# Scores of the large cross-attention stages from rounded keys and queries and their rests, in three passes

## The reference, cut to what matters

```python
q = (h @ Wq).reshape(B, N, 16, 64)        # h: layer norm of x, 112 tokens
k = (context @ Wk).reshape(B, S, 16, 64)  # 375 positions
v = (context @ Wv).reshape(B, S, 16, 64)
scores = einsum('bnhd,bshd->bhns', q, k) * scale
attn = softmax(scores)                    # over the 375 keys
x = x + einsum('bhns,bshd->bnhd', attn, v).reshape(B, N, 1024) @ Wo + bo
```

## Time and profile before

| | us |
|---|---|
| median of 3 runs | 1735.83 (1734.51 to 1738.16) |
| the profiled execution, its own time | 1738.72 |
| its span, first to last instruction | 1736.9 |
| mean granted clock of TensorE | 0.979 |

### The profile page before, as it was taken

One profiled execution on the slowest core, in us unless ns is written; L12 is line 12 of the kernel. 1 busy time (PEld: TensorE's weight loads), 2 busy tenths in 40 slices (PEclk: granted clock), 3 DMA queues, 4 the chain that ended last, 5 costly groups with the idle time before them and its releaser, 6 DMA issues.

```text
span 1736.9 us, 37112 instructions
## 1 busy us (share of the span) xinstructions
PE 1625.8 (94%) x13752; PEld 1378.1 (79%) x13752; DVE 978.4 (56%) x2648; ACT 1027.5 (59%) x2824; POOL 556.1 (32%) x1016
## 2 busy tenths in 40 slices
PE   5799999999989999999999979999999988999977
PEld 5788888888778888887888779888887777777757
DVE  6656644444656656644445555644455577767644
ACT  4456665566743556665556643555556676677771
POOL 3754333232221534333223220433223213443300
PEclk9899999999999999999999999999999999999989
DMA  4430210001110100210001110200101100111000
GB/s 131 148 113 31 66 33 14 14 15 52 42 36 29 62 1 26 72 33 15 15 14 41 42 43 30 67 17 15 28 15 48 52 17 4 32 30 31 2 4 19
DMA packets 37873, 65.07 MB, mean 37 GB/s; under 512 B 6784, under 2 KB 12384, under 8 KB 37696
## 3 DMA queue, kind: packets, MB, share of 16 engines
q1 hardware_dynamic: 37696, 62.70, 11.4%
HBM read 57.15 MB, written 5.54 MB: 36 GB/s over the span
## 4 chain that ended last, share of the span: by engine, by line
PE 81%; DVE 6%; ACT 6%; issue 3%; POOL 2%; DMA 1%; SPq 0%; DVEq 0%; POOLq 0%; ACTq 0%
PE pG L989 49%; PE pG L1119 12%; PE pS L989 10%; PE pO L989 10%; ACT L1309 1%; ACT P L1261 1%; DVE KF L1398 1%; ACT PT L1274 1%; ACT hid_lo_f L1309 1%; PE pG L1172 1%; DVE x L1441 1%; DMA V<-ctxT 1%; DVE bn L1324 1%; POOL P L1510 0%; DVE tmp L1439 0%
## 5 line engine op out<-in xcount | busy, mean ns | idle before, releaser
L1510 POOL TENSOR_SCALAR P<-P,rinv 112x375 f32<-112x375 f32 (+1 forms) x640 | 325.6, 520 | 565.6 <-DVE rinv L1404 565.3
L1261 ACT ACTIVATE P<-pS,nmax 112x375 f32<-112x375 f32 (+1 forms) x640 | 306.4, 492 | 212.4 <-DVE nmax L1380 212.2
L989 PE MATMUL pG<-hT_hi,W 128*128 128x224 f32 (+1 forms) x1408 | 336.5, 317 | 27.4 <-POOL hT_lo L1544 15.6
L989 PEld LDWEIGHTS pG<-hT_hi,W 128*128 128x128 f32 x1408 | 251.6, 201 | 38.4 <-issue 16.5
L1380 DVE TENSOR_REDUCE nmax<-pS 112x1 f32<-112x375 f32 (+1 forms) x448 | 229.3, 548 | 92.1 <-PE pS L989 91.7
L1274 ACT ACTIVATE PT<-pG 125x336 f32<-125x336 f32 (+1 forms) x448 | 208.0, 467 | 110.6 <-PE pG L1119 108.5
L1119 PE MATMUL pG<-ident,P 112*125 112x112 f32 (+1 forms) x1472 | 240.8, 277 | 18.0 <-POOL P L1510 8.4
L989 PE MATMUL pG<-src,W 128*128 128x376 f32 x1120 | 244.8, 349 | 0.3 <-DVE hid_hi_f L1357 0.3
L1119 PEld LDWEIGHTS pG<-ident,P 112*125 112x125 f32 (+1 forms) x1472 | 200.6, 176 | 53.7 <-issue 11.1
L989 PE MATMUL pG<-W,src 128*125 128x512 f32 x840 | 232.7, 410 | 1.0 <-DVE hid_lo_t L1365 0.7
L989 PE MATMUL pG<-hT_lo,W 128*128 128x224 f32 (+1 forms) x704 | 215.6, 306 | 0.0
(11 more groups left out here) (97 smaller groups left out, 2409.6 us busy)
## 6 DMA issues: line engine op xcount, KB each, us to landing
wraw<-wts SPq DMA_DIRECT2D x116, 256.0 KB, 2.5
src<-ctx_split SPq DMA_DIRECT2D x64, 282.0 KB, 3.0
ctx_split<-hid_lo_t SPq DMA_DIRECT2D x8, 564.0 KB, 4.0
V<-ctxT SPq DMA_DIRECT2D x8, 376.0 KB, 4.1
V<-wts SPq DMA_DIRECT2D x8, 256.0 KB, 3.4
bo_b<-bo SPq DMA_DIRECT2D x10, 112.0 KB, 2.7
out<-x SPq DMA_DIRECT2D x8, 112.0 KB, 1.8
x<-x_in SPq DMA_DIRECT2D x1, 672.0 KB, 5.5
```

The lines of the kernel that those rows point to most:

```text
L989: return nc.tensor.matmul(o, l, r, start=first, stop=last)
L1261: ins = act.activation(o, pS[U % 4][0:T, i * n:(i + 1) * n], ACT.Exp, bias=nmax[:, r, i:i + 1], accum_out=rsum[:, r, i:i + 1])
L1510: ins = pool.tensor_scalar(o, o, rinv[:, r, i:i + 1], st.nscale, ALU.mult, ALU.mult)
```

## The change

In stages 1 and 3, and in stage 4 from batch 2 on (`split`), the float32 score matmul of each head becomes three float32r matmuls: rounded queries with rounded keys, rounded queries with the keys' rest, the queries' rest with rounded keys. Only the product of the two rests is left out. For this

- VectorE copies a key tile from PSUM into a place for rests (`keys_rest`) instead of into `KF`; GpSimd rounds it into `KF_hi` (same memory as `KF`) and subtracts that in place;
- ScalarE scales a query tile into `queries_rest` instead of `QF`; VectorE rounds it into `QF_hi` (same memory as `QF`) and subtracts that in place (`ql`, two operations with a wait between);
- the rests lie in the feed-forward tiles, behind their tiles 0 and 1, so the first writes wait until these are free (`rest_free`), and hidden tiles 2 to 7 of the last batch wait until the sets that read the rests there are scored (`HID_FREE`);
- the pairs of hidden tiles in the last batch's four fills become 3, 1, 2 and 2;
- the planner's costs follow.

```diff
+def split(s, b):
+    return s in (1, 3) or s == 4 and b > 1
+HID_FREE = {0: 0, 1: 0, 2: 1, 3: 2, 4: 3, 5: 3, 6: 4, 7: 4}
...
-            for t in ((0, 1, 2), (3, 4), (5, 6), (7,))[i]:
+            for t in ((0, 1, 2), (3,), (4, 5), (6, 7))[i]:
...
-            return 1.25 if st.self_ else .7 if st.small else 1.75
+            return 1.25 if st.self_ else .7 if st.small else 1.2 if split(e.s, e.b) else 1.75
...
+        rest = nc.alloc_sbuf_tensor_at("rest", [128, 16 * CHUNK], F32R, offset=place)
+        whole_f = nc.alloc_sbuf_tensor_at("whole_f", [128, 16 * CHUNK], F32, offset=place)
...
+        def keys_rest(t, of=rest):
+            a = 2 * CHUNK + t // 2 * (SP + PAIR) + t % 2 * 8 * CHUNK
+            return of[:, a:a + SP]
+        def queries_rest(t, of=rest):
+            a = 2 * CHUNK + t // 2 * (SP + PAIR) + t % 2 * 8 * CHUNK + SP
+            return of[:, a:a + PAIR]
+        def rest_free(eng, s):
+            if s == 1:
+                wait(eng, ctx_out, 16 * B)
+            else:
+                wait(eng, pieces, piece_no[Ev("ff2", 1 if s == 3 else 3, B - 1)])
...
@@ tensor, set @@
-                                if st.small:
+                                if st.small or split(s, b):
                                     wait(pe, k_split, split_no[Ev("k", s, b, t)])
...
+                        if split(s, b):
+                            for p in range(3):
+                                for u in us:
+                                    t, r = sh.heads(u)[0]
+                                    rg = slice(rows * r, rows * (r + 1))
+                                    q = queries_rest(t)[rg, qc] if p == 2 else QF_hi[rg, t, qc]
+                                    k = keys_rest(t)[rg, :] if p == 1 else KF_hi[rg, t, :]
+                                    ins = mm(pS[u % 4][0:T, 0:SP], q, k, p == 0, p == 2)
...
@@ scalar, q @@
+                        if split(s, 2 * b):
+                            rest_free(act, s)
+                            o = queries_rest(e.i, whole_f)
+                        else:
+                            o = QF[:, e.i, :]
...
@@ scalar and vector, hidden tiles @@
+                    elif s < 6:
+                        rest_free(act, s)
+                        if HID_FREE[e.i]:
+                            wait(act, scored, scored_after(s, B - 1, 2 * HID_FREE[e.i] - 1))
...
@@ vector, k and ql @@
+                    elif split(s, b):
+                        wait(dve, scored, keys_free(s, b, e.i))
+                        rest_free(dve, s)
+                        dve.tensor_copy(keys_rest(e.i, whole_f), g[:, 0:SP]).then_inc(k_ready, 1)
...
+                    if not st.small:
+                        dve.tensor_copy(QF_hi[:, e.i, :], queries_rest(e.i, whole_f)).then_inc(q_hi, 1)
+                        dve.wait_ge(q_hi, q_hi_no[e])
+                        dve.tensor_tensor(queries_rest(e.i), queries_rest(e.i, whole_f), QF_hi[:, e.i, :].bitcast(F32),
+                                          ALU.subtract).then_inc(ql_ready, 1)
...
@@ gpsimd, k @@
+                    if s < 6:
+                        t = e.i
+                        pool.tensor_scalar(KF_hi[:, t, :], keys_rest(t, whole_f), 1.0, 1.0, ALU.mult, ALU.mult).then_inc(k_part, 1)
+                        pool.wait_ge(k_part, n)
+                        pool.tensor_tensor(keys_rest(t), keys_rest(t, whole_f), KF_hi[:, t, :].bitcast(F32), ALU.subtract).then_inc(k_split, 1)
```

More of the change, by code:

```diff
@@ L389, in duration @@
             return .62 if st.small else .6
-        return dict(ta=.75, tb=.68, hn=.42, ql=.36, w=.58, stat=.75, k=.55, qk=.72, norm=.15, wo=1.6, ff2=1.6, lnt=.78, ctx=.5, ffa=1.65, ffg=1.1)[k]
+        return dict(ta=.75, tb=.68, hn=.42, ql=.5, w=.58, stat=.75, k=.55, qk=.72, norm=.15, wo=1.6, ff2=1.6, lnt=.78, ctx=.5, ffa=1.65, ffg=1.1)[k]
     if k == "norm":
@@ L480, in plan @@
                 else:
-                    needs += [evicted(Ev("q", s, b // 2, t)), ("pool" if s == 6 else "dve", Ev("k", s, b, t))]
+                    needs += [("dve", Ev("ql", s, b // 2, t)) if s == 6 or split(s, b) else ("act", Ev("q", s, b // 2, t)), ("pool" if s == 6 or split(s, b) else "dve", Ev("k", s, b, t))]
             needs += [read(unit_no(s, b, u) - 4) for u in us if unit_no(s, b, u) > 3]
@@ L495, in plan @@
             task("act", e, ("pe", e))
-            if e.kind == "q" and s == 6:
+            if e.kind == "q" and (s == 6 or split(s, 2 * b)):
                 task("dve", e._replace(kind="ql"), ("act", e))
-        elif e.kind == "k" and s == 6:
+        elif e.kind == "k" and (s == 6 or split(s, b)):
             task("dve", e, ("pe", e))
@@ L651, in program @@
     ql_no = number(order["dve"], "ql")
+    q_hi_no = number([e for e in order["dve"] if e.s < 6], "ql")
     split_no = number(order["pool"], "k")
@@ L1097, in _ @@
                         bank_read(pe, unit(e, us[-1]) - 4)
-                        for i in range(sh.G if s < 6 else 0):
+                        if split(s, b):
[6 more added lines that the diff above has]
+                                    ins = mm(pS[u % 4][0:T, 0:SP], q, k, p == 0, p == 2)
+                        for i in range(sh.G if s < 6 and not split(s, b) else 0):
                             for u in us:
@@ L1475, in _ @@
                         wait(dve, pieces, piece_no[Ev("ff2", s, 3)])
-                    elif s == 3:
-                        wait(dve, pieces, piece_no[Ev("ff2", 1, B - 1)])
-                    elif s == 6:
+                    elif s < 6:
+                        rest_free(dve, s)
+                        if HID_FREE[e.i]:
+                            wait(dve, scored, scored_after(s, B - 1, 2 * HID_FREE[e.i] - 1))
+                    else:
                         dve.wait_ge(scored, scored_after(6, B - 1, 2 * (e.i - 4) + 1) if e.i > 3 else scored_after(6, B - 2, 7))
```

19 lines of the change are left out of this document (10 added, 9 removed).

## The result

The changed kernel takes 1756.5 us (median of four runs, 1755.6 to 1762.3) where the kernel before takes 1736.6 beside it: a ratio of 1.0122, 95% interval 1.0098 to 1.0147. It is slower by 20 us by the medians, 21 by the ratio; the forecast was faster by 20. The profiled execution is the one of 1762.3 us, 6 above the other three, so terms read from its trace come out somewhat large against the medians.

What follows compares the result with a forecast made beforehand. TensorE's own work was taken to bound the steady batches. Score sets -22.9, openings +2.8 and feed-forward pairs 0 sum to -20.1 us, from 1735.8 to 1715.7 us, range 1708 to 1728.

Steps and rivals of the forecast that it cites:

- The set: Score sets of stages 1, 3 and 4: 1.19 us each instead of 1.45, 22.9 us gained over 88 sets.
- The rival of the weight loads: Score sets: two weight loads per step go one after the other, step 187 ns, 1727.3 us; chance 0.08.
- The heads do run side by side: Score sets: the rival had heads not side by side in float32r, 2.26 us per set, 1810 us; chance 0.03.
- the third term: Last batch's feed-forward pairs, 3, 1, 2, 2: 0 us, between a gain of 2.5 and a loss of 3.2 per stage.
- the waits for hidden tiles: Last batch's feed-forward: hidden tiles wait for sets that TensorE has already gone through; cost nothing.
- The key copy keeps its form, only its target moves, and ScalarE's query eviction too: nothing.: Evictions from PSUM on VectorE and ScalarE in the converted stages: no added cost.
- Two covers: Converted stages: 7.3 us from norm to transpose and about 9 us from tile to set hide the splits.
- The sign of being right: Steady windows: TensorE stays over 99% busy and they get shorter by some 0.26 us per set.
- The query's split on VectorE: 88 query tiles, copy and subtraction within SBUF: 0.7 us each (0.4 to 0.85), 62 us in all, VectorE half idle.
- its GpSimd rival: Odd batches: key splits ahead of norms make GpSimd late, VectorE possibly held up to 1.0 us; 1773 us, chance 0.05.
- The openings: Last batches of stages 0 and 2: next stage's key splits delay norms, 2.8 us lost in all (0 to 6).
- the chance of 0.08 for slower: Whole kernel: chance of being slower by over 0.2%, about what a measurement can tell.

Runs made afterwards that it cites:

- the passes at the old costs: Kernel before with only the score sets as three float32r passes, rests left out, planner's old costs: 1715.2 us with old pairs, 1714.8 with new.
- old costs: Changed kernel with the planner's old cost of a set (1.75) and of the small stage's query rest (0.36): 1743.9 us, 1.0044.
- the deferrals: Changed kernel with query splits later in VectorE's order and the openings' key splits behind norms: 1733.7 and 1731.6 us; with the planner's old costs 1728.5.
- the passes alone: Changed kernel with both rests left out, no operation added, rounded tiles in all three passes, planner's new costs: 1729.4 us, 0.9955.
- ScalarE's order fixed: Changed kernel, query and opening key splits deferred, ScalarE emptying banks in TensorE's filling order: 1728.0 us with new planner costs, 1717.6 with old.
- queries deferred: Changed kernel with the queries' split later in VectorE's order, so that key copies pass it: 1743.0 us, 1.0041.
- The deferral: Changed kernel with the key splits of the openings of stages 1 and 3 behind the norms on GpSimd: 1751.7 us, 1.009.

## Why the prediction was wrong

**The set** was right: 1.21 us against 1.19, 22 us against 22.9. The rival of the weight loads is out. Its step was 187 ns, and the trace shows 170. The heads do run side by side, and the pairs cost nothing, as the third term had it. Nor do the waits for hidden tiles: of the two runs of the passes at the old costs the one with the new pairs has them, the other has neither, and they differ by 0.0003.

**"The key copy keeps its form, only its target moves, and ScalarE's query eviction too: nothing."** This is the first step that failed. Two covers had been looked at, from the norm to its transpose (7.3 us) and from the tile to its set (9 us), and both held: in the steady stretch of stage 1 no set and no transpose waited for a split. The cover that mattered was a third one. A tile leaves PSUM through one of a few `pG` banks, and TensorE wants the bank back within a fraction of a us. The copy kept its form but got a new neighbour: the query's cast and subtraction queue ahead of it. The sign of being right that was to show it, steady windows over 99% busy, failed: 216.28 of 224 us is 97%. The price list had VectorE's new work and the copy on separate lines, and no line for what stands behind the new work. The rule is to ask of each added operation what is queued behind it on its engine, and who waits for that.

**The query's split on VectorE** was also mis-sized. It was 0.7 us (0.4 to 0.85), and it measured 294 + 659 = 0.95 by the medians, 587 + 659 = 1.25 by the means. At rest the two take 0.25 + 0.39 = 0.64, so the estimate was right for an undisturbed VectorE, and the rest is GpSimd's hold, by its norms and roundings as well as by its subtraction. The prediction named that hold in its GpSimd rival, but gave it only late norms as a way to cost time. The norms of the odd batches were not late: in the steady stretch of stage 1 no wait of TensorE ended with one. The sign and the hold of that rival were right, its mechanism and its 1773 us were not. The +16 of the deferrals is these two steps and the openings: by the traces with the old costs some 9 us of it are the openings and 4 the batches 0 to 6 of the three stages; with the new costs it is 10 and 19.

**"The planner's costs follow"** is how the change described itself, and the prediction took no term for it at all. It measured 14 us in the changed kernel and 15 with the passes alone, but only 4 once both deferrals were in. The new 1.2 for a set is nearer to the chip's 1.21 than the old 1.75, and the order made from it is still worse. One part of the loss was found, banks emptied out of order: with the passes alone it is some 5 us in the odd batches. Not all: with ScalarE's order fixed the new costs are still 9 us behind (0.995 against 0.9897). The two traces, 13.8 us apart, place that: 11.7 lie in the last batches of stages 1 and 3 with their feed-forward. In that of stage 1 TensorE waited up to 1.37 us for a hidden tile's eviction and once 2.12 us for an exponential, and the granted clock from 430 to 480 us was 0.96 against 1.00. Which piece of the order causes these stays open.

**The openings** had 2.8 us (0 to 6), and this term was mis-sized. The profiled execution shows 11.8 for both, and two other traces with the key splits ahead of the norms show 9.7 (queries deferred) and 10.5 (old costs). The deferral brings 5.6 by the ratios when it is alone and 11 on top of the other one (1.0041 against 0.9976). So the openings cost some 10 us, more than the upper bound. Two norms were late instead of one. And with the wait of 2.91 us came the lower clock level for the work behind it, a cost of a wait that is not in its length and that the sum had not allowed for.

**What the range missed** is therefore above all three terms that weren't there: the turnaround of the banks, the order, and the clock after a wait. Of the chance of 0.08 for slower, 0.05 rested on the norms' slack and 0.03 on heads that don't run side by side; neither is what made the kernel slower in its steady batches.

## What to carry to other kernels

When TensorE is busy for over 99% of a stretch, look for the scarcest ring that feeds it, here a few PSUM banks with fractions of a us of slack: banks are to be emptied in the order in which they were filled, and everything that isn't urgent goes behind that, even where its engine is half idle. Where an order is planned from estimated costs, changing an estimate is a change of its own: measure the new instructions with the old order first, and don't expect truer estimates to give a better one. And where several losses share a wait, say in which order they were taken away: here one loss measured 14 us or 4, another 16 or 25.

## What the runs showed of the hardware

- **VectorE's work within SBUF is held until GpSimd's running instruction ends.** The query's cast takes 0.25 us when GpSimd stands still as it begins (30 of 88) and up to 1.07 us otherwise, its subtraction 0.39 and up to 1.17. All 41 casts over 0.4 us ended 0.13 to 0.14 us after a GpSimd instruction did: 28 after its subtraction, 10 after the rounding of a key tile, two after the layer norm's subtraction, one after a norm. Those 10, the longest, had begun during a norm and waited for it and the rounding behind it. Of the casts that began during the subtraction (36) the median is 965 ns. Without GpSimd's subtraction the longest cast is 0.37 us. With no new work on GpSimd at all (the queries' split without the keys') 8 casts still took 0.55 to 0.64 us, and all ended 0.13 us after a norm. The Trainium skill (SBUF — State Buffer, "Who interferes with whom") states this as an exclusive lock on a shared pair of ports; the trace agrees, with what is left of the other instruction as the price. An operation that reads PSUM instead (368 to 393 ns over all 88) showed no such hold.
- **Three passes on rounded operands, two heads side by side, take 0.17 us per step of 376 columns,** two weight loads of 112 columns included. The Trainium skill (TensorE: Matmul & The Clock Gate, "LDWEIGHTS (loading the stationary operand)") has a load last its columns over 1.2 GHz, by which each such load would take an estimated 93 ns. Were the two to follow each other, the step would be at least an estimated 187 ns; the trace doesn't show that.
- **The clock after a wait.** TensorE stood for 2.91 us, and the mean granted clock of the next 8 us was 0.60, part of them at the 1.2 GHz level; the same five passes took 1.79 instead of 1.02 us.
